# Gated-expert layer: the expert rows turned by DMA instead of by TensorE, the down projection two tiles behind, and a ring of seven weight slots

## The reference, cut to what matters

```
x = x + tanh(g_xattn[0]) * attention(layernorm(x), ctx)
h = layernorm(x)
logits  = h @ gate                       # 8 experts
top 2 of 8, softmax over the two  -> weights (the other six are 0)
y_n     = (silu(h @ w0[n]) * (h @ w1[n])) @ wo[n]     # 256 -> 512 -> 256
x = x + tanh(g_ffn[0]) * sum over n of weights[n] * y_n
```

## Time and profile before

| | |
|---|---|
| three runs, median (lowest to highest) | 1292.82 us (1287.88 to 1292.84) |
| profiled execution, first to last instruction | 1289.4 us |
| attention part and routing | to about 619 us |
| expert part, 135 tiles | 619 to 1289.4 us |

### The profile page before, as it was taken

The page is one execution under the profiler, slowest core; times in us unless marked ns, Lnnn a source line. Parts: engine busy times, 40 slices in busy tenths (PEclk is TensorE's granted clock), DMA queues, the critical chain, the costliest instruction groups (busy, mean ns, idle before and its releaser), DMA issues.

```text
span 1289.4 us, 35399 instructions
## 1 busy us (share of the span) xinstructions
PE 1216.0 (94%) x9926; PEld 1062.0 (82%) x9927; DVE 795.2 (62%) x2467; ACT 702.7 (54%) x1652; POOL 706.6 (55%) x1133
## 2 busy tenths in 40 slices
PE   4999999999999999981799999999999999999996
PEld 3899999999999999971688888888888888888884
DVE  4788888888888888864244444444444444444442
ACT  2788888888888888860233333333333333333332
POOL 2267777777777777765244444444444444444443
PEclk9899999999999999995799999999999999999998
DMA  5034444433433333375688733333333333333332
GB/s 157 30 129 146 140 143 143 136 136 135 137 129 127 128 122 132 133 239 192 170 217 208 200 54 55 54 53 53 57 53 53 57 53 55 55 53 53 57 54 33
DMA packets 73976, 139.71 MB, mean 108 GB/s; under 512 B 11605, under 2 KB 55157, under 8 KB 71765
## 3 DMA queue, kind: packets, MB, share of 16 engines
q1 hardware_dynamic: 39840, 86.05, 21.0%
q0 software_dynamic: 32064, 52.46, 20.7%
q10 hardware_dynamic: 2036, 0.75, 0.2%
HBM read 68.95 MB, written 70.27 MB: 108 GB/s over the span
## 4 chain that ended last, share of the span: by engine, by line
PE 47%; DMA 3%; issue 2%; POOL 1%; POOLq 0%; ACT 0%; DVE 0%; ACTq 0%; DVEq 0%
PE banks L1484 27%; PE psB L1500 9%; PE psB L1503 5%; PE psT L1492 4%; DMA out_dram<-ey,eid 2%; PE psG L1463 2%; DMA et<-routed_rows 1%; POOL w_part L493 0%; POOLq L538 0%; POOL routed_rows L487 0%; POOL out_dram L544 0%; ACT hgT L801 0%; DVE etT L1186 0%; POOL et L539 0%; ACT hs L795 0%
## 5 line engine op out<-in xcount | busy, mean ns | idle before, releaser
L1484 PE MATMUL banks<-w_all,etT 128*128 x1620 | 433.1, 403 | 0.7 <-ACT etT L789 0.7
L1484 PEld LDWEIGHTS banks<-w_all,etT 128*128 128x128 f32 x1620 | 286.7, 190 | 49.5 <-issue 1.1
L544 POOL DMA_INDIRECT out_dram<-ey,eid x135 | 216.5, 1604 | 178.0 <-DMA out_dram<-ey,eid 72.9
L1181 DVE TENSOR_TENSOR hgT<-psT,hgT 128x512 fp32r<-128x512 f32 x135 | 93.3, 691 | 259.3 <-ACT hgT L801 259.3
L539 POOL DMA_DIRECT2D et<-routed_rows x135 | 82.8, 613 | 205.2 <-issue 201.4
L807 ACT ACTIVATE ey<-psB,ewt 128x256 f32<-128x256 f32 x135 | 64.1, 475 | 226.1 <-PE psB L1503 226.1
L795 ACT ACTIVATE hs<-banks 128x512 f32<-128x512 f32 x135 | 80.7, 598 | 184.1 <-PE psT L1492 182.2
L487 POOL DMA_INDIRECT routed_rows<-rows,slot x128 | 127.0, 992 | 57.6 <-DVE slot L1020 28.9
L1317 PE MATMUL psB<-vbd,probT 128*128 128x51 f32 x1280 | 155.5, 269 | 0.0
L1317 PEld LDWEIGHTS psB<-vbd,probT 128*128 128x128 f32 x1280 | 152.9, 192 | 0.0
L1500 PE MATMUL psB<-w_all,hgT 128*128 x540 | 146.5, 393 | 0.8 <-ACT hgT L801 0.8
(11 more groups left out here) (163 smaller groups left out, 2295.9 us busy)
## 6 DMA issues: line engine op xcount, KB each, us to landing
split_weights<-w_part SPq DMA_DIRECT2D x16, 1536.0 KB, 6.2
w_all<-split_weights SPq DMA_DIRECT2D x32, 768.0 KB, 4.6
et<-routed_rows POOLq DMA_DIRECT2D x135, 129.0 KB, 2.4
xb<-in_x_dram SPq DMA_DIRECT2D x32, 256.0 KB, 3.4
w_raw<-in_L_ffn_w_kernel_dram SPq DMA_DIRECT2D x32, 256.0 KB
out_dram<-x SPq DMA_DIRECT2D x64, 128.0 KB, 1.7
w_raw<-in_L_ffn_wo_kernel_dram SPq DMA_DIRECT2D x16, 256.0 KB
cb<-in_ctx_dram SPq DMA_DIRECT2D x32, 77.0 KB
```

The costliest lines, as they stand in the source:

```text
L544: gp.indirect_dma_start(out=out, out_offset=bass.IndirectOffsetOnAxis(ap=eid[:, u:u + 1], axis=0), in_=ey[:, u % 2, :], in_offset=None, co ...
L1181: dve.tensor_tensor(hgT[:, 1].rearrange("p c q -> p (c q)"), psT[:], hgT[:, 0].rearrange("p c q -> p (c q)").bitcast(F32), ALU.subtract).t ...
L1484: m = pe.matmul(banks4[:, bank], etT[:, u % 2, a, c], weight(e, c, w, n), start=(j == 0), stop=(j == len(steps) - 1))
```

## The change

It has four parts.

1. **Turning by DMA.** For tiles 20 to 132 (T1 = 20, T2 = 133) PE's `g_T` is gone. DVE copies the 32-bit `hs` apart into two planes of 16-bit halves (`hs16`), SP issues a transposing DMA of 128 x 1024 halves (`hT16`), DVE joins the halves to words (`hT`), and the high and low parts are taken from there. Tiles 0 to 19, 133 and 134 still go through PE.
2. **Down projection two tiles behind** for the tiles turned by DMA (`downs`), one behind for the others. `hgT` gets a second buffer. POOL's adds run four tiles behind instead of two; `ey` still has two buffers.
3. **A ring of seven slots** in place of all eight experts' weights: expert 7 goes to expert 0's slot, fetched by ACT at tiles 64 and 66 (`fetch_last_up`, `fetch_last_down`). PE reads two registers for a tile's weights (`tup_i`, `tslot_i`) and a third before `down` (`tdown_i`), and waits for weights against registers.
4. **Adds wait less.** Two semaphores `added[0]`, `added[1]` by a tile's parity; an add waits for the add two before it, and for the one just before it only if that belongs to another expert or is padding. The count it needs comes from a table, `tadd_i`, read into a register. Seven small DVE instructions make the tables.

`tiles()` now has 24 peeled tiles, a loop, 8 peeled tiles, a loop and a rest, with 8 tiles a turn on every engine. The core of the diff:

```diff
+    SLOTS = E - 1
+    RING = SLOTS * DC
+    HALF_UP = NT
+    T1 = 20
+    T2 = MOE_T - 2
...
-        hgT = sb("hgT", [P, 2, FC, P], F32R)
+        hgT = sb("hgT", [P, 2, 2, FC, P], F32R)
+        hs16 = sb("hs16", [P, 2, 2, F], U16)
+        hT16 = sb("hT16", [P, 2, 2 * FC, P], U16)
+        hT = sb("hT", [P, FC, P])
...
+        def on_pe(t):
+
+            return isinstance(t, int) and (t < T1 or t >= T2)
...
+        def downs(t):
+
+            out = []
+            if known(t, 2) and not on_pe(t - 2):
+                out.append(2)
+            if known(t, 1) and on_pe(t - 1):
+                out.append(1)
+            return out
...
+            def turn_rows(t, u):
+
+                after(sp, (hs16_done, t - T1 + 1))
+                if known(t, T1 + 2):
+                    after(sp, (hT_done, t - T1 - 1))
+                sp.dma_start_transpose(hT16[:, u % 2], hs16[:, u % 2].rearrange("p s f -> p (s f)")).then_inc(hT_in[u % 2], 16)
...
+            def add_rows(t, u, q):
+
+                before = []
+                if known(t, 3):
+                    need = gp.value_load(tadd_i[0:1, bass.ds(t - 1, 1)], min_val=16, max_val=16 * MOE_T)
+                    before = [(added[(u - 1) % 2], need)]
+                elif known(t, 1):
+                    before = [(added[(u - 1) % 2], 16 * ((t + 1) // 2))]
+                if known(t, 2):
+                    before.append((added[u % 2], 16 * (q * (TURN // 2) + u // 2)))
+                after(gp, (ey_done, t + 1), (eid_done, 2 * (t + 1)), *before)
...
             def tile(t, u, q):
                 if below(t, MOE_T - 2):
                     load_rows(t + 2, u + 2)
-                if known(t, 2):
-                    add_rows(t - 2, (u - 2) % 4)
+                if known(t, 4):
+                    if not known(t, 5):
+                        gp.wait_ge(tab_done, 2)
+                    add_rows(t - 4, u - 4, q)
...
+            def h_high(t, u):
+                act.wait_ge(hT_done, t - T1 + 1)
+                high(t, u, hT[:].rearrange("p c q -> p (c q)"))
+
+            def y_evac(t, u, q):
                 act.wait_ge(ey_ps, t + 1)
                 if known(t, 2):
-                    act.wait_ge(added, 16 * (t - 1))
...
+                    act.wait_ge(added[u % 2], 16 * (q * (TURN // 2) + u // 2))
...
+            def fetch_last_up():
+
+                act.wait_ge(h1_ps, HALF_UP)
+                act.wait_ge(w_in, 16 * 2 * RING)
+                for q in last_q:
+                    for part in range(2):
+                        act.dma_start(w_all[:, q % RING, part, 0:2].rearrange("p r f -> p (r f)").bitcast(F32),
+                                      split_w[q][:, part * QW:part * QW + 2 * F]).then_inc(w_in, 16)
+
+            def fetch_last_down():
+
+                act.wait_ge(ey_ps, HALF_UP)
+                act.wait_ge(w_in, 16 * 2 * NQ)
...
                 silu(t, u)
-                if known(t, 1):
-                    g_evac(t - 1)
+                for lag in downs(t):
+                    if lag == 1:
+                        g_evac(t - 1, u - 1)
+                    else:
+                        h_high(t - 2, u - 2)
                 if below(t, MOE_T - 1):
                     e_evac(t + 1, u + 1)
-                if known(t, 1):
-                    y_evac(t - 1, (u - 1) % 4)
+                for lag in downs(t):
+                    y_evac(t - lag, u - lag, q)
...
+            def halves(t, u):
+
+                dve.wait_ge(hg_done, t + 1)
+                if known(t, T1 + 2):
+                    dve.wait_ge(hT_done, t - T1 - 1)
+                dve.tensor_copy(hs16[:, u % 2], hs[:].bitcast(U16).rearrange("p (f s) -> p s f", s=2)).then_inc(hs16_done, 1)
+
+            def words(t, u, q):
+
+                dve.wait_ge(hT_in[u % 2], 16 * (q * (TURN // 2) + u // 2 + 1 - T1 // 2))
+                if known(t, T1 + 1):
+                    dve.wait_ge(hgT_lo, t)
+                dve.tensor_copy(hT[:].bitcast(U16).rearrange("p c (q s) -> p s c q", s=2), hT16[:, u % 2].rearrange("p (s c) q -> p s c q", s=2)).then_inc(hT_done, 1)
...
-            def down(t, e):
+            def down(t, u, e):
+                need = pe.value_load(tdown_i[0:1, bass.ds(t, 1)], min_val=2 * 16 * DC, max_val=2 * 16 * (NQ + DC))
+                pe.wait_ge(w_in, need)
                 pe.wait_ge(hgT_hi, t + 1)
...
-            def expert_with_weights(t):
-
-                e = pe.value_load(texp_i[0:1, bass.ds(t, 1)], min_val=0, max_val=E - 1)
-                pe.wait_ge(w_in, (e + 1) * (DC * 2 * 16))
-                return e
+            def expert_of(t):
+
+                need = pe.value_load(tup_i[0:1, bass.ds(t, 1)], min_val=2 * 16 * DC, max_val=2 * 16 * NQ)
+                e = pe.value_load(tslot_i[0:1, bass.ds(t, 1)], min_val=0, max_val=SLOTS - 1)
+                return e, need
...
+                pe.wait_ge(w_in, weights_need[u])
                 pe.wait_ge(etT_hi, t + 1)
...
-                if known(t, 1):
+                if known(t, 1) and on_pe(t - 1):
                     g_T(t - 1)
...
-                if known(t, 1):
-                    down(t - 1, expert[u - 1])
+                for lag in downs(t):
+                    down(t - lag, u - lag, expert[u - lag])
```

More of the change, by code:

```diff
@@ L10 @@
 U32 = mybir.dt.uint32
+U16 = mybir.dt.uint16
 ALU = mybir.AluOpType
@@ L397, in _ @@
             for done in (*scattered, tab_done):
-                sp.wait_ge(done, 32 * NT // 4 if done is not tab_done else 1)
+                sp.wait_ge(done, 32 * NT // 4 if done is not tab_done else 2)
             for done in et_in:
@@ L402, in _, with tile @@
             sp.wait_ge(split_out, 16 * NQ)
-            for q in range(EARLY, NQ):
+            for q in range(EARLY, RING):
                 for part in range(2):
                     fetch_part(q, part)
+            def turn_rows(t, u):
[3 more added lines that the diff above has]
+                sp.dma_start_transpose(hT16[:, u % 2], hs16[:, u % 2].rearrange("p s f -> p (s f)")).then_inc(hT_in[u % 2], 16)
+            def tile(t, u, q):
+                if not on_pe(t):
+                    turn_rows(t, u)
+            tiles(sp, tile)
         @block.gpsimd
@@ L803, in y_evac, with high, g_evac @@
-            def y_evac(t, u):
+            def high(t, u, src):
+                if known(t, 2):
+                    act.wait_ge(ey_ps, t - 1)
+                act.copy(hgT[:, u % 2, 0].rearrange("p c q -> p (c q)"), src).then_inc(hgT_hi, 1)
+            def g_evac(t, u):
+                act.wait_ge(hgT_ps, through_pe(t))
+                high(t, u, psT[:])
+            def h_high(t, u):
+                act.wait_ge(hT_done, t - T1 + 1)
+                high(t, u, hT[:].rearrange("p c q -> p (c q)"))
@@ L804, in y_evac @@
+            def y_evac(t, u, q):
                 act.wait_ge(ey_ps, t + 1)
                 if known(t, 2):
-                    act.wait_ge(added, 16 * (t - 1))
-                act.activation(ey[:, u % 2], psB[:, D:2 * D], ACT.Copy, scale=ewt[:, u:u + 1]).then_inc(ey_low, 1)
+                    act.wait_ge(added[u % 2], 16 * (q * (TURN // 2) + u // 2))
+                act.activation(ey[:, u % 2], psB[:, D:2 * D], ACT.Copy, scale=ewt[:, u % 4:u % 4 + 1]).then_inc(ey_low, 1)
+            last_q = range((E - 1) * DC, NQ)
@@ new lines, in fetch_last_up @@
+            def fetch_last_up():
[8 more added lines that the diff above has]
+                act.wait_ge(w_in, 16 * 2 * NQ)
+                for q in last_q:
+                    for part in range(2):
+                        act.dma_start(w_all[:, q % RING, part, 2].bitcast(F32), split_w[q][:, part * QW + 2 * F:(part + 1) * QW]).then_inc(w_in, 16)
@@ L1528, in tile @@
                 if below(t, MOE_T - 1):
-                    expert[u + 1] = expert_with_weights(t + 1)
-                    if u == UNROLL - 1:
-                        pe.reg_mov(next_expert, expert[u + 1])
-                        pe.reg_mov(last_expert, expert[u])
-                if known(t, 1):
+                    expert[u + 1], weights_need[u + 1] = expert_of(t + 1)
+                    if u == TURN - 1:
+                        pe.reg_mov(carried_need, weights_need[u + 1])
+                        pe.reg_mov(carried["next"], expert[u + 1])
+                        pe.reg_mov(carried["last"], expert[u])
+                        pe.reg_mov(carried["second_last"], expert[u - 1])
+                if known(t, 1) and on_pe(t - 1):
                     g_T(t - 1)
                 if below(t, MOE_T - 1):
-                    e_T(t + 1, u + 1, (q * UNROLL + u + 1) // 2 if isinstance(q, int) else q * (UNROLL // 2) + (u + 1) // 2)
+                    e_T(t + 1, u + 1, q * (TURN // 2) + (u + 1) // 2)
                 up(t, u, expert[u], 1, 2 + u % 2, h1_ps)
-                if known(t, 1):
-                    down(t - 1, expert[u - 1])
-            UNROLL = 8
-            tiles(pe, tile, unroll=UNROLL)
+                for lag in downs(t):
```

(4 more changed lines are left out.)

158 lines of the change are left out of this document (98 added, 60 removed).

## The result

The changed kernel takes **1451.15 us** (median of four runs, 1446.46 to 1457.48) against 1291.59 us for the kernel before (four runs, 1287.88 to 1292.84): a ratio of **1.125**, 95% interval 1.1222 to 1.1271. The forecast was 1420 us with a range of 1360 to 1500.

A forecast was written before the change was run, and what follows sets the result against it. PE was taken to bound the kernel at 4.84 us a tile. Terms of 81 + 41 + 5 + 2 = +129 us on the 1292.8 us median gave about 1420 us, range 1360 to 1500.

The forecast's parts named there:

- PE's saving is gone before anything else: On PE's sequencer, three register loads of 0.8 us a tile instead of one put its floor at about 4.8 us.
- Tiles 2 to 19, +81: Loop through POOL's read and add, landing, ACT and DVE spans one tile: 9.6 us against 4.84, +81 us.
- Tiles 20 to 132, +41: Loop through read, add, landing, `y_evac`, `words` spans two tiles: 10.4 us, 5.2 a tile against 4.84, +41 us.
- POOL's load, taken at 0.5: Register load between POOL's read and add, taken as 0.5 us of the loop, bounds 0 and 0.8.
- Rival C: DVE's `words` and `halves` copy one element a cycle, 1.2 for 0.7 us: +0.25 a tile, 1448 us; chance 0.08.
- The turning, taken at 4 to 5 us and free: Transposing DMA from issue to landing takes 4 to 5 us; up to 6.5 us it costs nothing.
- rival A: The transposing DMA lands late, at 8 us: beat 5.95, 125 us in place of 41, 1504 us; chance 0.17.
- Rival B: POOL's reads and adds start up to 0.7 us later behind DVE's copies: +0.35 a tile, 1460 us; chance 0.1.
- Rival D: PE's granted clock falls in tiles 2 to 19: up to +20 us, 1440 us; chance 0.1.
- Expert 7, +5: ACT waits in tile 66 for weights issued in tile 64: 2 to 3 us stall plus slower landings, +5 us.
- Rival E: Adds hold up nothing at `y_evac`; PE bounds: 1295 us, or 1250 if register loads hide; chance 0.04 in all.
- At nothing, the freed adds: Adds no longer waiting for each other gain nothing: their chain costs about 4.7 us a tile, under 4.84.

The follow-up runs named there:

- the ring cut: Changed kernel with adds three instead of four tiles behind: 1307.1 us; or with four `ey` buffers instead of two: 1300.2 us.
- doubling: Changed kernel with POOL's register load before each add done twice: 1487.2 us.

## Why the prediction was right

The sum was +129 us and the spans differ by 155.5; the sign, the place of the loss and its mechanism were as forecast, and one term, the ring of tiles 20 to 132, makes the difference.

**PE's saving is gone before anything else** held, though PE's floor was never reached in the change. With the ring cut the beat was 4.80 to 4.84, as the 4.8 to 4.9 from the earlier trace rows said, and one load instead of three gave 4.44. That the number fits at three loads is in part luck: the same sum with two loads is about 4.1, so that 4.40 would have held, and 4.58 was measured. "Between the two the larger holds" was too simple, and a load was taken too dear: 0.8 in the sum, 0.22 and 0.14 us of the beat in the runs.

**Tiles 2 to 19, +81.** Measured +78.6; a quiet beat is 9.3 (9.6 in the sum). Followed through the trace of tiles 3 to 16, the ring is 9.37 us in the mean. Two errors of the sum cancel in part, which is luck: from the add to `y_evac` it is 4.00 where 3.85 was taken, from the read to the add 1.44 for 1.66. The adds two, three and four behind in the changed kernel, and three and four behind in the one before, settle the mechanism.

**Tiles 20 to 132, +41.** This is the term that was mis-sized: the 108 tiles from 22 to 130 lost 70.4 us, 7 of them to expert 7. The loop was read as 10.4 us and is 10.62 in the round shown above, 5.31 a tile. Followed through the trace over 92 rounds of the same tiles that the beat is taken from, its mean is 10.85, and half of that is the beat of 5.42: 1.54 to the read (1.42 in the sum), 1.71 to the add (1.66), 4.03 to `y_evac` (3.85), 0.93 to `words` (0.99), 0.84 for `words` and wake (0.75), 0.65, 0.61 and 0.54 (0.61, 0.61 and 0.53). So +0.58 for +0.36 a tile is a sum of small shares, the largest being the landing and the first leg. The first leg did not grow with the change: over tiles 25 to 129 it is 1.53 in the median before and 1.57 after, and the tile of the earlier trace rows with its 1.42 was one of the shortest. The landing of 8.7 us belongs to the tiles beside expert 7's fetch, which the beat leaves out. The landings from 1070 to 1400:

```profile
DMA to landing us min/median/max: 3.7/3.9/4.4
```

**POOL's load, taken at 0.5** between 0 and 0.8: 0.44 to 0.51 by doubling. **DVE's copies, taken at 0.7**: 698 and 750 ns. Rival C falls.

**The turning, taken at 4 to 5 us and free.** It landed in 3.0 to 6.3, median 3.5 us, under the 6.5 from which it would have counted; rival A falls: in the change `words` never waited more than 0.2 us for it. In the kernels with the ring open or shorter it did come once each, beside expert 7's fetch in one block, with a wait of 5.1 to 12.2 us.
By the figure of the Trainium skill, "VectorE: DVE Perf Modes", section on the three transpose paths, 1309 ns for a 128x128 block, the eight blocks would have made the estimated 10.5 us one behind the other; this trace does not agree: eight blocks in one instruction land in 3.5.

**Rival B**, POOL held by a copy, is there, but small. Two adds that start while `words` runs:

```profile
1099.65 0.75 DVE L1307 COPY hT<-hT 128x1024 uint16<-128x1024 uint16 x1
1099.69 2.15 POOL L605 DMA_INDIRECT out_dram<-ey,eid  x1 [1.16 <-PE psG L1594]
...
1105.03 0.74 DVE L1307 COPY hT<-hT 128x1024 uint16<-128x1024 uint16 x1
1105.46 1.76 POOL L605 DMA_INDIRECT out_dram<-ey,eid  x1 [1.04 <-DVE ey L1321]
```

The first finds 0.71 us of the copy left and takes 2.15 us, the second finds 0.31 left and takes 1.76; both end 1.44 to 1.45 us behind the copy's end. So it is throughout: 62 of the 135 adds start while `words` runs, and the 58 of them that find more than 0.16 us of it left end 1.43 to 1.45 us behind its end, whatever was left. The 50 adds that meet neither copy take 1.60 in the mean, as in the kernel before, and 18 of the 23 in which a copy starts later take 1.60 or 1.61 too (the other five 1.70 to 2.04). So an add that finds the copy running waits for the rest of it, less 0.17 us. The mean over all adds is 1686 ns. In the quiet stretches from 900 to 1400 the held adds land 4.02 us behind their start, the others 3.82, and half of the adds are held: about 0.1 a round, 0.05 of the rival's 0.35 a tile.
This agrees with the lock that the Trainium skill, "SBUF — State Buffer", section "Who interferes with whom", describes, by which whichever of the two starts first holds the shared port. No run here takes the copy away.

**Rival D** came in part: with PE busy in 42.5 of 65 us the granted clock was 0.84 in the mean of that stretch, so between its levels of 1.2 and 2.4 GHz, and 0.88 in the kernel before with adds four behind. It cost nothing that can be seen: the early ring passes through ACT without waiting for PE (in the early turn above `silu` starts 0.37 us behind `y_evac`), and a quiet early beat of 9.3 us is not above the loop's own length.

**Expert 7, +5**: about 7 in the change, but not by the wait that the forecast named: ACT's longest idle time there is 6.49 us for the landing of an add, which took up to 8.7 us beside the 2 MB. **Tail, +2**: 3.6. **Rival E** fell with the waits: the landing is what `y_evac` waited for.

**At nothing, the freed adds.** Right for the change, but the chain of adds, read as 4.7 us, stood only 0.1 under PE's beat; where PE needs 4.44 it sets 4.86 in the mean.

## What to carry to other kernels

Before moving a step by whole tiles, follow the ring through every queue it stands in and count how many tiles it spans: its length divided by that count is a floor on the beat, and a queue position is worth as much as a buffer. In such a ring, work saved elsewhere is worth nothing (32 us became 0) and every latency added is paid in full, divided by the tiles it spans. Put loads, waits and transfers where the beat has room only after the ring is open; and ask of each bound how far behind it the next one stands.

## What was not expected of the hardware

Register loads on PE's sequencer are not of one length. From 1000 to 1200 in the changed kernel the load for `down` (L1629) against its first and last start:

```profile
L1629 PEldq TENSOR_LOAD <-tdown_i x35: 298/336/697, 1003.5 to 1196.4; - x35
```

With four `ey` buffers the same load had a median of 622 ns and reached 838, while the load of the slot number, a few instructions away, stayed at a median of 299. What it meets there was not found, nor whether it bears on the beat.

The turning DMA was late beside plain transfers: with four `ey` buffers and one load, behind 2 MB in large pieces on another queue its issue took 6.46 us instead of 1.23 and its landing 10.7 instead of 3.5, while the same bytes spread over seven tiles cost 3 us in place of 14.

An add on POOL that starts while DVE's `words` runs ends 1.44 us behind the copy's end, to within 0.02 us, whatever was left of the copy, if that was more than 0.16 us (58 adds in the change); an add that meets no copy takes 1.60 in all.
